# A graph-transformer layer on one core: second attention products beside the next group's first scores, last two projections in the next group

## What is computed

```python
nx = _layernorm(x, ln1_g, ln1_b)
q, k, v = (nx @ W + b for W, b in ((Wq, bq), (Wk, bk), (Wv, bv)))
scores = einsum('bqhd,bkhd->bhqk', q, k) / sqrt(HEAD_DIM)
scores = where(adj_mask[:, None, :, :], scores, NEG)
out = einsum('bhqk,bkhd->bqhd', softmax(scores), v) @ Wo + bo
x = x + out
nx = _layernorm(x, ln2_g, ln2_b)
return x + gelu(nx @ W1 + b1) @ W2 + b2
```

## Time and profile before

| | |
|---|---|
| median of 3 runs | 2147.41 us (2147.28 to 2148.95) |
| the profiled execution's own time | 2148.58 us |
| its span | 2146.6 us |
| PE busy | 2125.0 us (99%) |
| DVE busy | 1490.7 us (69%) |
| ACT busy | 905.0 us (42%) |
| POOL busy | 431.6 us (20%) |
| share of PE in the chain that ended last | 96% |
| mean granted clock of PE | 0.998 |

### The profile page before, as it was taken

One profiled execution on the slowest core, in us unless ns is written; L12 is line 12 of the kernel. 1 busy time (PEld: TensorE's weight loads), 2 busy tenths in 40 slices (PEclk: granted clock), 3 DMA queues, 4 the chain that ended last, 5 costly groups with the idle time before them and its releaser, 6 DMA issues.

```text
span 2146.6 us, 33138 instructions
## 1 busy us (share of the span) xinstructions
PE 2125.0 (99%) x13216; PEld 1754.3 (82%) x13216; DVE 1490.7 (69%) x2211; ACT 905.0 (42%) x1321; POOL 431.6 (20%) x293
## 2 busy tenths in 40 slices
PE   8999999999999999999999999999999999999999
PEld 6888888888888877888888888888888888888887
DVE  5888888888999966666666666666666656666333
ACT  4444444433344444435335335335345345345332
POOL 2233434321111224004004004003003003003200
PEclk9999999999999999999999999999999999999999
DMA  6344333431222116336445445444444544544532
GB/s 188 111 155 135 134 134 134 146 117 66 70 76 70 46 56 231 150 140 223 170 156 206 168 173 190 177 181 179 187 181 171 196 180 167 201 165 172 211 129 92
DMA packets 103842, 323.98 MB, mean 151 GB/s; under 512 B 21409, under 2 KB 29601, under 8 KB 87329
## 3 DMA queue, kind: packets, MB, share of 16 engines
q1 hardware_dynamic: 98192, 321.68, 40.9%
q10 hardware_dynamic: 5520, 0.55, 0.2%
HBM read 265.57 MB, written 56.62 MB: 150 GB/s over the span
## 4 chain that ended last, share of the span: by engine, by line
PE 96%; DVE 3%; DMA 0%; ACT 0%; issue 0%; POOL 0%; SPq 0%; DVEq 0%; ACTq 0%
PE lin L180 11%; PE lin L182 10%; PE lin L181 10%; PE ps_r L180 5%; PE ps_r L182 5%; PE ps_r L181 5%; PE ps_x L180 5%; PE ps_x L182 5%; PE ps_out L182 5%; PE ps_x L181 5%; PE ps_out L181 5%; PE ps_out L180 5%; PE ps_z L182 3%; PE ps_z L181 3%; PE ps_z L180 3%; PE lin L1425 1%
## 5 line engine op out<-in xcount | busy, mean ns | idle before, releaser
L1209 DVE TENSOR_TENSOR acc<-ps_r,acc 128x512 f32<-128x512 f32 x256 | 176.4, 689 | 329.7 <-PE ps_r L182 329.0
L817 ACT ACTIVATE snaps<-ps_x 128x512 f32<-128x512 f32 x192 | 114.3, 596 | 410.1 <-PE ps_x L182 410.0
L180 PE MATMUL ps_r<-w_ring,h_ring 128*128 128x512 f32 x512 | 199.5, 390 | 0.7 <-DVE h_ring L1199 0.6
L180 PE MATMUL ps_x<-nxc,w_ring 128*128 128x512 f32 x512 | 199.4, 389 | 0.0
L181 PE MATMUL ps_x<-nxc,w_ring 128*128 128x512 f32 x512 | 199.2, 389 | 0.0
L182 PE MATMUL ps_r<-w_ring,h_ring 128*128 128x512 f32 x512 | 199.2, 389 | 0.0
L182 PE MATMUL ps_x<-nxc,w_ring 128*128 128x512 f32 x512 | 199.2, 389 | 0.0
L181 PE MATMUL ps_r<-w_ring,h_ring 128*128 128x512 f32 x512 | 199.2, 389 | 0.0
L180 PE MATMUL ps_out<-w_ring,h_ring 128*128 128x512 f32 x512 | 199.2, 389 | 0.0
L182 PE MATMUL ps_out<-w_ring,h_ring 128*128 128x512 f32 x512 | 199.2, 389 | 0.0
L181 PE MATMUL ps_out<-w_ring,h_ring 128*128 128x512 f32 x512 | 199.2, 389 | 0.0
(11 more groups left out here) (137 smaller groups left out, 5056.7 us busy)
## 6 DMA issues: line engine op xcount, KB each, us to landing
w_ring<-w_scratch SPq DMA_DIRECT2D x64, 1792.0 KB, 7.3
w_ring<-w_scratch SPq DMA_DIRECT2D x64, 1024.0 KB, 7.1
xb<-x_scratch SPq DMA_DIRECT2D x22, 1024.0 KB, 10.1
xres<-in_x SPq DMA_DIRECT2D x64, 256.0 KB, 3.4
x_scratch<-xres SPq DMA_DIRECT2D x64, 256.0 KB, 2.1
x<-in_x SPq DMA_DIRECT2D x15, 1024.0 KB, 6.0
acc<-x_scratch SPq DMA_DIRECT2D x32, 256.0 KB, 2.9
out<-xb SPq DMA_DIRECT2D x32, 256.0 KB, 2.0
```

What stands on the lines that cost most here:

```text
L180: pe.matmul(out, lhs[1], rhs[0], start=first, stop=False, skip_group_check=resumed)
L817: act.activation(snaps[:, j], ps_x[:, :], ACT.Copy).then_inc(snap_done[j], 1)
L1209: dve.tensor_tensor(acc(t), ps_r[:, :], acc(t), ALU.add).then_inc(acc_added, 1)
```

## The change

**Order.** S0 leaves a group's own list. A new kind `("Z", 0)`, `score(g + 1, ...)`, stands at the end of the list of the group before, right behind O1. W2 and W3 leave the list too; a new kind `("X", t)`, `project(g - 1, t, ...)`, stands as X2 and X3 behind U0 of the next group's list (group 0 has none). EARLY_ORDER is the list of group 14, LAST_ORDER that of group 15.

**What follows it.** ACT's `att_hi(g, 1)`, DVE's `att_lo(g, 1)` and `residual(g, 2)`, `residual(g, 3)`, POOL's `bias_xres(g, 3)` and SP's `store_x1(g, 1..3)` and `load_xres(g, 3)` move into the body of the next group. DVE's transposes for group g+2 stand in other pieces (0 to 6, 6 to 10, 10 to 13, 13 to 16). In the last group ACT does both exponents ahead of the first `take_probT`.

In the diff below the bodies come in the order SP, POOL, ACT, DVE, PE.

**Group 1's input** is transposed by DVE (`ln_transpose(1, 1, 0, 16)`), no longer by PE; kind T is gone.

```diff
-ORDER = [("S", 0), ("U", 0), ("U", 1), ("U", 2), ("U", 3), ("P", 0), ("U", 4), ("U", 5),
...
+ORDER = [("U", 0), ("X", 2), ("X", 3), ("U", 1), ("U", 2), ("P", 0), ("U", 3), ("U", 4), ("U", 5), ("S", 1), ("O", 0),
+         ("U", 6), ("U", 7), ("W", 0), ("U", 8), ("P", 1), ("U", 9), ("U", 10), ("U", 11), ("W", 1), ("O", 1), ("Z", 0)]
...
+EARLY_ORDER = [("U", 0), ("X", 2), ("X", 3), ("U", 1), ("P", 0), ("U", 3), ("U", 4), ("S", 1), ("O", 0), ("U", 6), ("U", 7),
+               ("W", 0), ("P", 1), ("U", 9), ("U", 10), ("W", 1), ("O", 1), ("Z", 0)]
+LAST_ORDER = [("L", 2), ("X", 2), ("S", 1), ("X", 3), ("L", 5), ("L", 8), ("P", 0), ("L", 11), ("O", 0), ("F", 1), ("F", 5),
+              ("P", 1), ("W", 0), ("W", 1), ("O", 1), ("F", 6), ("F", 2), ("W", 2), ("F", 7), ("W", 3)]
...
-        units = [("U", j) for j in FIRST_UNITS]
-        return units[:-3] + [("T", k) for k in range(KC)] + units[-3:] if g == -1 else []
...
+        return [("U", j) for j in FIRST_UNITS] + [("Z", 0)] if g == -1 else []
...
             def body(g, par):
+                if g > 0:
+                    store_x1(g - 1, 1)
+                    load_xres(g - 1, 3)
...
+                if g > 0:
+                    store_x1(g - 1, 2)
+                load_xres(g, 0)
+                if g > 0:
+                    store_x1(g - 1, 3)
+                load_xres(g, 1)
...
             def last_body(g):
...
                 conv_lo(0)
+                bias_xres(g - 1, 3)
                 pool.wait_ge(shifted, PAIRS * g + 1)
                 conv_lo(1)
...
             def last_body(g):
+                att_hi(g - 1, 1)
                 for n in range(4):
                     conv_hi(0, n)
                 exponent(g, 0)
+                exponent(g, 1)
                 take_probT(g, 0)
-                exponent(g, 1)
...
             def body(g, par):
+                if g > 0:
+                    att_lo(g - 1, 1)
                 mask_and_shift(g, par, 0)
...
+                if g > 0:
+                    residual(g - 1, 2)
                 normalise(g, 0)
+                if g > 0:
+                    residual(g - 1, 3)
...
+            ln_transpose(1, 1, 0, QUADS * QUADS)
...
                     elif kind == "W":
                         project(g, n, take_bank(g, "W", n))
+                    elif kind == "X":
+                        project(g - 1, n, take_bank(g, "X", n))
                     else:
-                        transposes(g + 2, par, n, take_bank(g, "T", n))
+                        score(g + 1, 1 - par, n)
```

More of the change, by code:

```diff
@@ L113, in order_of @@
 def order_of(g):
-    if isinstance(g, int) and g < 0:
-        units = [("U", j) for j in FIRST_UNITS]
-        return units[:-3] + [("T", k) for k in range(KC)] + units[-3:] if g == -1 else []
+    if not isinstance(g, int):
+        return ORDER
+    if g < 0:
+        return [("U", j) for j in FIRST_UNITS] + [("Z", 0)] if g == -1 else []
     if is_last(g):
         return LAST_ORDER
[L119 to L123, removed]
+    if g == NG - 2:
+        return EARLY_ORDER
+    return [(k, n) for k, n in ORDER if g > 0 or k != "X"]
 def units_through(g, j):
@@ L134, in lin_uses @@
 def lin_uses(g):
-    return [(g, k, j) for k, n in order_of(g) if k in "UTOWL" for j in ((2 * n, 2 * n + 1) if k == "O" else (n,))]
+    return [(g, k, j) for k, n in order_of(g) if k in "UOWXL" for j in ((2 * n, 2 * n + 1) if k == "O" else (n,))]
 def ring_place(g, kind, n):
@@ L146, in ring_place @@
     at = [u[1:] for u in uses].index((kind, n))
-    assert len(uses) % LIN == 0 and len(lin_uses(-2) + lin_uses(-1) + lin_uses(0)) % LIN == 0
-    return at % LIN, uses[at - LIN] if at >= LIN else (g - 1, *uses[at - LIN][1:])
+    before = sum(len(lin_uses(i)) for i in (-1, 0))
+    assert len(uses) % LIN == 0
+    return (before + at) % LIN, uses[at - LIN] if at >= LIN else (g - 1, *uses[at - LIN][1:])
 def bank_of(g, kind, n):
@@ L361, in load_x @@
             def load_x(g, par):
[L363 to L366, removed]
+                if g == 2:
+                    sp.wait_ge(t_done, KC)
+                elif g > 2:
+                    sp.wait_ge(z_transposed, g - 2)
                 sp.dma_start(x[par][:, :, :], x_groups[g]).then_inc(x_loaded[par], 16)
@@ L467, in body @@
                     load_acc(0, 1)
-                store_x1(g, 2)
-                store_x1(g, 3)
+                    store_x1(g, 2)
+                    store_x1(g, 3)
             def load_xb(part):
@@ L693, in affine @@
                 source = z1T[:, k]
[L694 to L697, removed]
+                if g == 0:
+                    source = first_t[k]
+                    act.wait_ge(t_done, k + 1)
                 else:
-                    act.wait_ge(z_transposed, g - 1)
+                    act.wait_ge(z_transposed, g)
                 act.activation(z1T[:, k], source, ACT.Identity, scale=cols[:, 0, k:k + 1],
@@ L765, in body @@
                 unit(9)
-                att_hi(g, 1)
-                unit(10)
+                if g < PREP:
+                    job_hi(g, 2)
                 if "N" in kinds_of(g):
@@ L770, in body @@
                         affine(g + 2, k)
+                unit(10)
+                if "N" in kinds_of(g):
                     for k in range(KC):
@@ L1338, in take_bank @@
                         pe.wait_ge(which, KC * (i + 1) + n // 3 + 1)
-                    elif kind == "T":
-                        pe.wait_ge(which, KC * (i + 2) + n + 1)
                     elif kind == "O":
@@ L1343, in take_bank @@
                     else:
-                        pe.wait_ge(which, TILES * i + n + 1)
+                        pe.wait_ge(which, TILES * (i - (kind == "X")) + n + 1)
                 return lin[bank]
-            def transposes(g, par, k, bank):
-                pe.wait_ge(zn_done, TILES * (g + 1))
-                for t in range(TILES):
-                    mm = pe.transpose(bank[:, t * P:(t + 1) * P], x[par][:, t, k * P:(k + 1) * P], ident[:, :])
-                mm.then_inc(t_done, 1)
             def unit(g, j, bank):
```

75 lines of the change are left out of this document (28 added, 47 removed).

## The result

The changed kernel took **2174.71 us** in the median of four runs (2172.10 to 2175.16), the kernel before 2147.35 beside it: ratio 1.0125 [1.011, 1.014], 27 us slower. Forecast were 2163.5 us and a range of 2154 to 2169. The direction held, the size did not. The profiled execution's own time was 2175.16, its span 2173.0; before, 2146.6.

What follows compares the result with a forecast made beforehand. PE, busy 99% of the span, was taken as the bound. Terms -3.7, -1.7, +1.1, +18.1, -0.5, +7.5 and -4.3 sum to +16.5 us on 2148.6; adjusted to the median, the forecast was 2163.5 us, range 2154 to 2169.

Steps and rivals of the forecast that it cites:

- The loop's end (+18.1): PE's loop over groups 1 to 12: five jumps back, behind small blocks, each leave PE idle 3.6 us ahead of U0, +18.1 us.
- Clock (+7.5): Behind the five jump pauses PE's granted clock falls, costing 1.5 us a jump, +7.5 us.
- Rival 2: The jump shows but the clock holds, so without the 7.5 us: 2156 us; chance 0.10.
- Joined blocks (-3.7): O1 of groups 0 to 14 joined with the next group's S0 saves 0.24 us, 15 times: -3.7 us.
- The -0.5 for the old jumps: The few tenths by which S0 started late at the five jumps before the change go, estimated -0.5 us.
- Group 1's transposes and P0 (-1.7, +1.1): At the start, moving group 1's transposes off PE gives -1.7 us; P0 of group 0 newly waits for prob, +1.1 us.
- Steady groups (0): In the steady groups attT_lo, prob and nx_split still come in time for PE, so no change: 0 us.
- Rival 3: A steady group also waits, for attT_lo or prob, 0.5 us in 14 groups: 2171 us; chance 0.06.
- Last two groups (-10.8, +4.8, +1.7): Group 14's waits and their slow clock go, -10.8 us; in the last group O0 waits for probT, +4.8, slow clock +1.7.
- Rivals 1 and 4: Jump doesn't show, faster, 2138 us, chance 0.09; jump costs half, 1.8 us each, 2148.5 us, chance 0.04.

## Why the prediction was right and wrong

**The loop's end (+18.1): right in mechanism, too small.** The loop now ends in small blocks that cover next to nothing of the jump. Moving the jump in both kernels and writing the loop out show it. The step that failed is "the branch will ... run 3.5": I carried the duration of the earlier trace rows over as if it were the branch's own. It is its length with quiet DMAs (3.29 to 3.76 us), and the change put the transfers of the new body's start beside it (3.96 to 6.08 at the first three jumps). I had listed those transfers for POOL's bias, and not asked what they run into. The idle time came to 22.6 us in this profile and 19.5 in the second. With the DMAs quiet it was 17.4, so the term was right for what it assumed, and its upper bound, 19 us from the longest of the earlier trace rows, was a bound over quiet jumps only.

**Clock (+7.5): right in kind, 9.0 measured.** I had put up to 1.7 us on a fall and taken 1.5. The longer periods less their idle time give 1.5 to 1.7 for four of them, and 2.4 for the one behind the six-us pause, since its slow stretch was longer. In the second profile and with all transfers held back, 7.4 and 8.7 are left of the longer periods when the idle time and the waits for attT_lo in them are taken off. Rival 2 (the clock holds) is out, though behind one pause of 3.5 us in the second profile the clock did hold (1.00).

**Joined blocks (-3.7): 0.19 instead of 0.24 a group.** I priced the new pair O1, S0 with the rows of S1, O0 (2.34); it costs 2.43 in the loop. Written out it would have saved more than I took. The difference makes 0.7 us of the error over thirteen groups. The -0.5 for the old jumps held: the five periods with one were 0.7 longer in sum before the change.

**Group 1's transposes and P0 (-1.7, +1.1): both held, one wait was missing.** U0 started at 50.66 for a predicted 50.8, P0 waited 0.91 for 1.1. The -1.7 came out by some luck: the first scores started 2.2 us earlier, and 0.4 of that went to a longer wait for nxT_lo. Not counted was the wait of W0 for attT_lo, 0.68 (77.71 us). I had followed P0 and stopped there, although W0 of group 0 also lacks the cover of X2 and X3. Group 1 waits 0.3 there too.

**Steady groups (0): right.** No wait for attT_lo, prob or nx_split in groups 2 to 13 of this profile (one of 0.2 in the second); the periods without a jump agree within 0.02 us. Rival 3 is out. How thin that cover is shows in the kernel with the pair apart.

**Last two groups (-10.8, +4.8, +1.7): -2.8 behind group 13's mark instead of -4.3 and -0.5 for two pairs.** Group 14 has no wait, as forecast. O0 waited 6.1 us instead of 4.8. "One more bias ... now stands between" was right, but the difference beside it took

```profile
833.05 3.37 POOL L599 TENSOR_TENSOR nxc<-bT,nxc 128x1024 fp32r<-128x1024 f32 x1
836.35 0.95 POOL L552 MEMSET softmax<- 128x1024 f32 x1
```

3.37 and the one ahead of the bias 3.39 us, 6.8 together, where the two took 5.7 before and I had kept the old distance between the fills. The slow clock behind it lasted six microseconds (844.7 to 850.8, above) for a cost of 3.0 where I had 1.7. And 1.0 more for h_ring, in the MLP, I had not looked at; in the second profile that wait is 0.7, so it scatters.

**The sum.** Measured less predicted, on this profile: 9.9 us. By the marks 0.9 of it lies ahead of group 0's, 7.0 between the marks and 2.0 behind group 13's. Between them branches 4.5, clock 1.5, pairs 0.7 and attT_lo 0.3 make 7.0. Ahead of them attT_lo gives 0.7. Behind them the wait of O0 (1.3), its clock (1.3) and h_ring (1.0) make 3.6; the 1.6 too much I can't place. The second profiled execution of the same program had a span of 2167.4, 5.6 shorter, 3.1 of it idle time at the jumps: so this term has a spread that no single profile gives, and the range of 2154 to 2169 should have had room above for it. All eight executions of the changed kernel lie above 2169 (2169.54 to 2176.0). Rivals 1 and 4 are out: the branch took 0.21 us in the MLP's loop again, but in this one never under 3.29.

**The jump in the Trainium skill.** The trace contradicts the 108 ns of the Trainium skill, Advanced Engine Details and Errata (Control Flow Timing), in every taken jump of this loop, and comes near in the last one, which falls through (83 ns). The account in the Trainium skill, Runtime: NRT & Kernel Launch (Instruction fetch mechanics), that a jump's target is fetched first if it isn't held, agrees with the packet of the instruction queue that each of the taken branches has in it. That the kernel's own transfers can delay this packet is shown by the classes above and by its place in the first three jumps. Why the MLP's loop takes its jumps in 0.21 us wasn't tried.

## What to carry to other kernels

Where a hardware loop jumps back is part of the schedule: put the boundary behind a long run of large products (36 here), not behind small blocks, and price it as idle time plus the slow clock behind it. A duration read from a trace holds for the surroundings it was read in; ask of a fetch, as of any transfer, what the change starts beside it. And where a last group waits, follow the whole chain (copies, v, weights, fill): taking one link out of it only renamed the wait.

## What was not expected of the hardware

- The same taken branch took 3.29 to 3.76 us with quiet DMAs and 3.96 to 6.08 with busy ones, and differed by up to 1.9 us between two executions of one program.
- A pair of small blocks of 64 products each cost 2.43 us in the loop and 2.24 written out. Why the second block starts 0.15 us later in the loop wasn't tried.
- The slow stretch at a pause wasn't of one length, and the pause's length didn't settle it. Added up from the granted clock, it was 3.4 us at the four pauses of 4.0 to 4.4 us in the changed kernel's first profile and 6.8 at the two of 6.0 and 6.1, of which 1.9 and 0.7 lie inside the pause. In its second profile it was 6.8 at a pause of 4.3 us, and behind one of 3.5 the clock held.
